# Decoder layer in fp32: cross-attention probabilities and values exchanged between partitions through DRAM instead of inside SBUF, with the division moved

## What is computed

```python
        sim = jnp.einsum('bhid,bjd->bhij', q, k) + mask[:, None, :, :]
        attn = jax.nn.softmax(sim, axis=-1)
        out = jnp.einsum('bhij,bjd->bhid', attn, v)
        out = out.transpose(0, 2, 1, 3).reshape(b, n, INNER) @ Wout
        h = xn @ W1
        val, gate = jnp.split(h, 2, axis=-1)
        out = out + jax.nn.silu(gate) * val @ W2
```

## Time and profile before

| | |
|---|---|
| median of 3 runs | 2093.75 us (2090.76 to 2095.71) |
| profiled execution | 2093.83 us |
| its span, first to last instruction | 2092.0 us |
| TensorE busy | 1724.8 us (82%) |
| VectorE busy | 1346.2 us (64%) |
| ScalarE busy | 974.7 us (47%) |
| DMA engines, mean busy share | 37.1% |

### The profile page before, as it was taken

How to read it: one execution, slowest core, us unless ns; L and a number is a source line. 1 busy time by engine, 2 the same in 40 slices (tenths; PEclk the granted TensorE clock), 3 DMA queues, 4 the chain that set the end, 5 groups by cost and what they waited for, 6 DMA issues and landing times. The chain is left out here.

```text
span 2092.0 us, 25897 instructions
## 1 busy us (share of the span) xinstructions
PE 1724.8 (82%) x7880; PEld 908.4 (43%) x7880; DVE 1346.2 (64%) x3972; ACT 974.7 (47%) x2262; POOL 419.4 (20%) x569
## 2 busy tenths in 40 slices
PE   5579999999996668878878877887888787888786
PEld 2447676676663223333333333333433333333355
DVE  6888999899656555655466465556646656564643
ACT  3355445544335455445455544545544554453541
POOL 4867686768500100000000000000000000000000
PEclk8789999999997879989899989999999999899998
DMA  3000000000144654545454554544554455454531
GB/s 126 1 18 10 27 10 27 19 28 2 35 147 117 185 125 118 130 103 127 121 130 108 142 117 116 133 118 120 124 127 112 117 125 128 107 124 116 118 82 37
DMA packets 153005, 197.33 MB, mean 94 GB/s; under 512 B 56513, under 2 KB 113793, under 8 KB 151969
## 3 DMA queue, kind: packets, MB, share of 16 engines
q1 hardware_dynamic: 152400, 195.21, 37.1%
q10 hardware_dynamic: 464, 0.46, 0.1%
HBM read 96.92 MB, written 7.42 MB: 50 GB/s over the span
## 5 line engine op out<-in xcount | busy, mean ns | idle before, releaser
L1749 ACT ACTIVATE x_pr<-x_pr,x_mx 128x375 f32<-128x375 f32 x448 | 268.3, 599 | 493.4 <-DVE x_mx L1875 493.4
L1875 DVE CUSTOM_DVE_ANT_0 x_pr<-ps,x_mk 128x375 f32<-128x375 f32 x448 | 227.4, 545 | 266.0 <-issue 141.8
L1554 PE MATMUL ps<-x_xn,x_w 128*128 128x448 f32 x512 | 255.1, 634 | 89.8 <-DVE x_so L1962 37.6
L1755 ACT ACTIVATE x_pr<-x_pr,x_rc 128x375 f32<-128x375 f32 x448 | 244.2, 592 | 4.1 <-DVE x_rc L1881 4.1
L1530 PE MATMUL ps<-x_pT,x_va 128*64 128x512 f32 (+1 forms) x768 | 176.6, 600 | 65.5 <-DMA x_pT<-x_blk 65.5
L1892 DVE STREAM_TRANSPOSE x_blk<-x_pr 128x384 f32<-128x384 f32 x448 | 227.8, 547 | 0.0
L1513 PE MATMUL ps<-x_kT,x_qT 64*128 64x375 f32 x896 | 208.7, 545 | 2.6 <-issue 2.4
L1554 PEld LDWEIGHTS ps<-x_xn,x_w 128*128 128x128 f32 x512 | 103.4, 216 | 211.3 <-issue 99.9
L314 PE MATMUL ps<-m_xa,w_in 128*128 128x448 f32 x352 | 146.5, 564 | 6.2 <-ACT m_xa L532 6.2
L1905 DVE TENSOR_TENSOR x_cT<-x_cT,x_rb 128x375 f32<-128x375 f32 x64 | 32.0, 541 | 163.9 <-DMA x_rb<-context_roots 163.9
L1554 PE MATMUL ps<-f_xn,f_w 128*128 128x448 f32 x224 | 100.4, 577 | 39.3 <-DVE x_ff L1947 21.0
(11 more groups left out here) (194 smaller groups left out, 2817.3 us busy)
## 6 DMA issues: line engine op xcount, KB each, us to landing
x_pT<-x_blk SPq DMA_DIRECT2D x512, 96.0 KB, 2.1
x_mk<-in_mask SPq DMA_DIRECT2D x224, 187.5 KB, 4.5
x_pT<-x_blk SPq DMA_DIRECT2D x512, 72.0 KB, 2.1
x_cx<-in_context SPq DMA_DIRECT2D x32, 375.0 KB
x_cT<-in_context_turned SPq DMA_DIRECT2D x32, 375.0 KB, 5.1
x_rb<-context_roots SPq DMA_DIRECT2D x32, 187.5 KB, 5.3
x_va<-x_vT SPq DMA_DIRECT2D x256, 12.0 KB, 1.8
m_Rd<-bc_roots SPq DMA_DIRECT2D x8, 448.0 KB, 3.5
```

The source lines that it names most:

```text
L1554: last = pe.matmul(to[:, 0:T], weights[:, k, at:at + 128], moving[:, k, :], start=(k == 0), stop=(k == KD - 1))
L1749: act.activation(pr[:, k, 0:J], pr[:, k, 0:J], ACT.Exp, scale=-1.0, bias=mx[:, k:k + 1], accum_out=sums[:, k:k + 1]).then_inc(h_e.sem, 1)
L1755: act.activation(pr[:, k + e, 0:J], pr[:, k + e, 0:J], ACT.Copy, scale=rc[:, k + e:k + e + 1]).then_inc(h_n.sem, 1)
L1875: dve.tensor_tensor_reduce(pr[:, k + e, 0:J], bank(2 * (p % 2) + e)[:, 0:J], mk[:, p % SLOT, :], -1.0, 3.0e38, ALU.add, ALU.min, mx[:, k + ...
```

## The change

- The blocks that VectorE turned no longer go from SBUF to SBUF. `blocks_out(p - 2)` stores each step's blocks to a DRAM buffer with one DMA (128 partitions x 4 runs of 768 bytes), and `blocks_in(p - 3)` loads a batch back with four DMAs (32 partitions x 4 runs of 3072 or 2304 bytes each). `blocks` becomes a ring of 3 steps, and `pT` and the DRAM buffer have two copies, so that a load waits for the V product before the last one only.
- The values take the same way: 2 stores (`values_out`, at r = 6) and 2 loads (`values_in`, at r = 0 of the next context) in place of 8 DMAs.
- VectorE's order in a step becomes `highest(p)`, `turn(p - 1)`, the pieces, `divide(p)`; ScalarE's `scaled(p - 1)`, `exps(p)`, the pieces. So the turn comes one step earlier.

```diff
-        def turned_across(i, p):
+        def blocks_out(i, p):
+
+            m = i * STEPS + p
+            sp.wait_ge(h_t.sem, h_t.value(i, 2 * p + 2))
+            if p % NP in (0, NV):
+                hold(sp, h_o, i, batch(p) - 1)
+            sp.dma_start(turned_dram[batch(p) % NB][:, :, p % NP % NV, :].rearrange("q p x -> p q x"),
+                         blocks[:, m % STAGES, :].rearrange("p (q x) -> p q x", q=RB)).then_inc(l_ps[m % STAGES].sem, 16)
+
+        def blocks_in(i, p):
             if p % NP not in (NV - 1, NP - 1):
                 return
...
+            for k in range(p - STAGES + 1, p + 1):
+                told(sp, l_ps, i, k)
+            hold(sp, h_o, i, n - 1)
+            for q in range(RB):
+                sp.dma_start(pT[n % NB][BLK * q:BLK * q + BLK].rearrange("p r s t w b -> p r (s t w b)"),
+                             turned_dram[n % NB][q].rearrange("(r a) s x -> a r (s x)", a=BLK)).then_inc(l_pt.sem, 16)
...
+                if p >= 2 or not first:
+                    blocks_out(*back(it, p, 2))
                 if p >= 3 or not first:
-                    turned_across(*back(it, p, 3))
+                    blocks_in(*back(it, p, 3))
...
         def group(it, first=False, last=False):
             for p in range(STEPS):
-                exps(it, p)
                 if p >= 1 or not first:
                     scaled(*back(it, p, 1))
+                exps(it, p)
...
         def turn(i, p):
...
+            m = i * STEPS + p
+            told(dve, l_ps, 0, m - STAGES)
+            to = blocks[:, m % STAGES, :].rearrange("p (c w b) -> p c w b", w=2, b=BLK)
...
                 highest(it, p)
                 if p >= 1 or not first:
-                    divide(*back(it, p, 1))
-                if p >= 2 or not first:
-                    turn(*back(it, p, 2))
+                    turn(*back(it, p, 1))
...
+                divide(it, p)
```

More of the change, by code:

```diff
@@ L1060 @@
 LAG = 5
-PARTS = RB * RB
+SW = 2 * JW
 CONTEXT = (0, 1, 4)
-VPARTS = DH // BLK * RB
+VPARTS = DH // BLK
+STAGES = 3
 CROOT = 2 * JT + 1 + RSQRT
@@ L1187, in norm_apply, with attention @@
         dve.tensor_scalar(dst(b), src(b), mv[:, b, 0:1], y[:, b:b + 1], ALU.subtract, ALU.mult).then_inc(done.sem, 1)
-def attention(nc, ctx0, PS, apart, ident, xm_dram, ctx_dram, ctx_turned, roots_dram, mask_dram, out_dram, w):
+def attention(nc, ctx0, PS, apart, ident, xm_dram, ctx_dram, ctx_turned, roots_dram, turned_dram, values_dram, mask_dram, out_dram, w):
     sb = Arena(nc, ARENA_AT)
@@ L1220, in attention @@
     rc = sb("x_rc", [ROWS, 2 * SLOT])
-    blocks = [sb(f"x_blk{n}", [ROWS, JW * 2 * width]) for n, width in enumerate((NV, NP - NV))]
-    pT = sb("x_pT", [128, JW * 2 * NV])
+    blocks = sb("x_blk", [ROWS, STAGES, SW])
+    pT = [sb(f"x_pT{n}", [128, RB, width, JC, 2, BLK]) for n, width in enumerate((NV, NP - NV))]
     OT = [sb("x_OT0", [128, GB, KA * S])]
@@ L1255, in attention @@
     c_t = count("c_t", GB)
-    l_pt = count("x_lpt", 16 * PARTS * NB * GB)
+    l_ps = [count(f"x_lps{n}", 0) for n in range(STAGES)]
+    l_pt = count("x_lpt", 16 * RB * NB * GB)
+    l_vs = count("x_lvs", 16 * VPARTS * GB)
     l_rs = count("x_lrs", 16 * GB)
@@ L1328, in batch, with told @@
         return p // NP * NB + p % NP // NV
-    def width_of(n):
-        return 2 * (NV if n % 2 == 0 else NP - NV)
+    def told(eng, sems, i, p):
+        m = i * STEPS + p
+        if m >= 0:
+            eng.wait_ge(sems[m % STAGES].sem, 16 * (m // STAGES + 1))
     def half(ap, h):
@@ L1389, in turned_in, with values_out @@
             sp.dma_start(cT[:, :, :], ctx_turned[i * GB + b, :, :].rearrange("(k p) j -> p k j", p=128)).then_inc(l_ct.sem, 16)
+        def values_out(i, b):
+            sp.wait_ge(c_t.sem, c_t.value(i, b + 1))
+            for k in range(DH // BLK):
+                sp.dma_start(values_dram[:, :, k, :].rearrange("q y x -> y q x"),
+                             vT[BLK * k:BLK * k + BLK, :].rearrange("p (q x) -> p q x", q=RB)).then_inc(l_vs.sem, 16)
         def values_in(i, b):
-            sp.wait_ge(c_t.sem, c_t.value(i, b + 1))
+            sp.wait_ge(l_vs.sem, l_vs.value(i, 16 * VPARTS * (b + 1)))
             hold(sp, h_o, i, NB * (b - 1))
             for k in range(DH // BLK):
-                for q in range(RB):
-                    sp.dma_start(va[BLK * q:BLK * q + BLK, b % 2, :, BLK * k:BLK * k + BLK],
-                                 vT[BLK * k:BLK * k + BLK, q * JC * BLK:(q + 1) * JC * BLK].rearrange("p (t d) -> p t d", d=BLK)).then_inc(l_va[b % 2].sem, 16)
-        def turned_across(i, p):
+                sp.dma_start(va[:, b % 2, :, BLK * k:BLK * k + BLK],
+                             values_dram[:, :, k, :].rearrange("q y (t x) -> (q y) t x", x=BLK)).then_inc(l_va[b % 2].sem, 16)
+        def blocks_out(i, p):
[6 more added lines that the diff above has]
+        def blocks_in(i, p):
             if p % NP not in (NV - 1, NP - 1):
@@ L1445, in group @@
                 b, r = divmod(p, NP)
+                if r == 0 and not (first and b == 0):
+                    values_in(it, b)
                 if last and b == GB - 1:
@@ L1485, in sync @@
         tokens_out(LAST - 2)
+        values_out(0, 0)
         values_in(0, 0)
@@ L1490, in sync @@
         group(NG - 1, last=True)
-        turned_across(NG - 1, STEPS - 1)
+        for p in (STEPS - 2, STEPS - 1):
+            blocks_out(NG - 1, p)
+            blocks_in(NG - 1, p - 1)
+        blocks_in(NG - 1, STEPS - 1)
         for h in range(2):
@@ L1883, in turn @@
         def turn(i, p):
[L1885 to L1889, removed]
+            m = i * STEPS + p
+            told(dve, l_ps, 0, m - STAGES)
+            to = blocks[:, m % STAGES, :].rearrange("p (c w b) -> p c w b", w=2, b=BLK)
             for e in range(2):
                 dve.wait_ge(h_n.sem, h_n.value(i, 2 * p + e + 1))
-                dve.transpose(to[:, :, 2 * (r % NV) + e, :], pr[:, 2 * (p % SLOT) + e, :].rearrange("p (c b) -> p c b", b=BLK)).then_inc(h_t.sem, 1)
+                dve.transpose(to[:, :, e, :], pr[:, 2 * (p % SLOT) + e, :].rearrange("p (c b) -> p c b", b=BLK)).then_inc(h_t.sem, 1)
         def context_norm(it, b, stage):
@@ L2057, in vector @@
         group(NG - 1, last=True)
-        turn(NG - 1, STEPS - 2)
+        turn(NG - 1, STEPS - 1)
         end_back(0)
-        divide(NG - 1, STEPS - 1)
         end_norm(0, 0)
-        turn(NG - 1, STEPS - 1)
         end_norm(0, 1)
@@ L2078, in program @@
     roots = nc.dram_tensor("context_roots", (JP, JT), FP32, kind="Internal").ap()
+    turned_blocks = [nc.dram_tensor(f"turned_blocks{n}", (RB, ROWS, width, JC * 2 * BLK), FP32, kind="Internal").ap() for n, width in enumerate((NV, NP - NV))]
+    turned_values = nc.dram_tensor("turned_values", (RB, BLK, DH // BLK, JC * BLK), FP32, kind="Internal").ap()
     with ExitStack() as ctx:
@@ L2085, in program @@
         mix = mixer(nc, ctx, PS, ident, i_in, x, xm, bc_roots, w)
-        att = attention(nc, ctx, PS, apart, ident, xm, ctx_dram, ctx_turned, roots, mask_dram, out, w)
+        att = attention(nc, ctx, PS, apart, ident, xm, ctx_dram, ctx_turned, roots, turned_blocks, turned_values, mask_dram, out, w)
         block = ctx.enter_context(nc.Block())
```

7 lines of the change are left out of this document (3 added, 4 removed).

## The result

The change makes the kernel faster: 1956.97 us median of 4 runs (1951.0 to 1963.72) against 2093.28 us, ratio 0.935 (95% interval 0.9308 to 0.9392), 136 us. The forecast was 1927 us, with 1860 to 2015 as its range: right in sign and 30 us too low, and the mechanism that it put first, SyncE's issue time, turned out to be about half of the gain.

What follows compares the result with a forecast made beforehand. The prediction took SyncE's issue time to close the loop that holds most contexts, with TensorE busy 80% in the steady part. Its terms summed as 2093.8 - 82 - 50 - 15 - 20 = 1927 us, range 1860 to 2015.

Steps and rivals of the forecast that it cites:

- SyncE's issue time closes the loop: In SyncE's queue, issuing 16 exchange DMAs takes 10.08 us; the loop of 41.7 us holds most contexts of 44.7 us.
- Term 1: The context's roots through DRAM: they leave earlier, saving 82 of TensorE's 100.5 us of waits, bounds 25 to 110.
- lands at about 1293: In one context, `roots_out` could go at 1287.1, queues behind the second batch's four loads, and lands at about 1293 us.
- the round trip stays: Rival: bursts of loads and stores ahead of the roots keep three quarters of the roots' saving away; 2009 us, chance 0.12.
- Term 2: TensorE's wait for exchanged probabilities (`x_pT`) before the products: loads land 2 to 4 us earlier, saving 50 of 65.5 us.
- products wait for their DRAM pair: Rival: store and load through DRAM take 1.9 us more on 64 products, 122 us; 2049 us, chance 0.06.
- Term 3: New order on VectorE and ScalarE: scaling fills ScalarE's idle time, tanh comes up to 1.1 us earlier, saving 15 us.
- a store is a step old by then: In SyncE's queue, the new wait ahead of the loads holds back `roots_out`, but stores land in 3.7 us, steps average 6.4.
- Term 4: TensorE's clock after stalls, 0.63, taken as halfway between two levels: 24 stalls with about 1 us slower matmuls, 20 us saved.
- The DMA engines: DMA busy time per context rises from 22.3 to 32.4 us, a share of 0.82 in 39.5 us, called high, yet hidden.
- the DMA rival: Rival: stores at 110 ns per 768-byte packet make the DMA engines the bound and the kernel slower; 2167 us, chance 0.08.
- Lockstep: Rival: VectorE's `turn` waits for `scaled` wherever ScalarE is behind, 0.3 us x 224 = 67 us; 1994 us, chance 0.05.

Runs made afterwards that it cites:

- the order alone: The kernel before with only the new order on VectorE and ScalarE, the exchange untouched: 2071.88 us, ratio 0.9917.
- Exchange alone: The changed kernel with the old order on VectorE and ScalarE put back, exchange and values still through DRAM: 2168.6 us, ratio 1.0395.
- small masks: The changed kernel with mask loads cut to 8 of 375 columns after the first four: 1921.78 us, ratio 0.9199.

## Why the prediction was right, and where it was off

- *SyncE's issue time closes the loop.* Right as a bound that the change removed: putting twelve issues a batch back costs 74 us. The estimate of 9.5 us of issue per context holds: 7 stores at 0.39, 8 loads in two runs of 2.1, four DMAs of about 0.5 make 8.9. Not right as the only thing: with 16 issues a batch the new route and order still gained 66 us.
- *Term 1, 82 us; measured 49.6.* This is the term that was too large. The step at fault is "lands at about 1293": 6 us for `roots_out` behind the loads. It took 8.5 in the rows above, and in total SyncE waits 182.2 us for it. (The step's own sum also gives 1298.3 and 0.6 us, not 1299 and 1.6, which changes little.) That the loads ahead are what holds up the small store is shown twice. With `roots_out` ahead of them SyncE's wait falls to 23.7 us, and the values' stores of 48 KB land in 8.2 us behind four loads and in 1.9 us behind sixteen. The context issued behind it is not the cause: with that moved away SyncE still waits 189.5 us. What in the four loads takes the 2.5 us more stays open. The forecast of the wait itself, under 50, was missed: 70.0. The rival "the round trip stays" holds in part, with 0.4 of term 1 lost, not three quarters.
- *Term 2, 50 us; measured 39.1.* Wait for `x_pT` 26.4, forecast under 25. The time was sized well: 7.2 us for a load to land, and 2.05 us for the four issues, make at most 9.3 from the first issue on, inside the 8.5 to 10.5. But the four issues are not what gave it. With sixteen the wait is 31.6 us already, and with the order alone 64.4, so most of this term belongs to the route and not to the number of DMAs. The rival "products wait for their DRAM pair" did not come in the changed kernel. A wait of that size came with the old order (189.1 us), and there the late turn is the nearer reading, since the changed kernel has the same pair and waits 26.4. The section that the rival names (the Trainium skill, DMA: Bandwidth & Descriptors, Anatomy of one DMA) describes DMAs issued by gpsimd, and all of these are SyncE's. No run here took a receipt apart.
- *Term 3, 15 us.* 18 us alone. But I called the order a small term of its own, and in the arrangements tried it is a condition of the exchange: without it the route costs 79 us. The sentence "a store is a step old by then" rested on the early turn, and I never priced the exchange without it.
- *Term 4, 20 us; measured 44.2.* The sign was right and the size half. The granted clock of 0.63 is not halfway between the two levels (0.5 and 1) but the mean of a stretch: 0.50 from 1214 to 1216 us and 0.76 from 1216 to 1219. The same four matmuls before and after that stall:

```profile
1202.99 1.67 PE L1554 MATMUL ps<-x_xn,x_w 128*128 128x448 f32 x4
1213.85 3.35 PE L1554 MATMUL ps<-x_xn,x_w 128*128 128x448 f32 x4 [5.69 <-DVE x_so L1962]
```

  They lost 1.7 us, not "about 1", and TensorE's 27 waits for products were left out of the count. See also the last section.
- *The DMA engines.* 32.4 us a context forecast; (1777.8 - 810.4) / 24 = 40.3 us a context, from the first and last `roots_out` of 25 between 800 and 1800 us, x 0.79 = 31.8. The price of 45 ns a packet fits: 31.8 - 22.3 = 9.5 us for 224 packets, 42 ns, if the loads cost what the exchange inside SBUF did, which no row tells by itself. The rule of the Trainium skill, Perfetto Trace Analysis, DMA Optimizations, on DMAs under 2 KB did not decide here. It speaks of the size of a DMA; these stores have 384 KB each, in runs of 768 bytes, and the engines did not become the bound that the DMA rival named. "High, yet hidden" was the wrong word all the same, as the smaller masks show.
- *Lockstep* did not show: VectorE waits 1.7 us in all ahead of the transposes for ScalarE.

Against the span, 49.6 + 39.1 + 44.2 = 132.9 of 142.8 us. Term 3 has no share of its own in that, since what the order gave lies in these waits. Of the rest, 4.1 is TensorE's wait behind the gate piece (47.6 before, 43.5 after).

## What to carry to other kernels

Where one queue issues every transfer, add its issue durations around a loop before looking at bytes: 16 small DMAs of 0.63 us were dearer here than a detour through DRAM with twice the bytes, and half of the gain came only when four DMAs did the loading. Then ask what leaves the queue's wait: the queue that was no longer busy issued in bursts, and a short round trip behind a burst took the burst's time. Five reorderings of the transfers were tried, one in the kernel before and four in the changed one. Each lengthened one wait at least, and all four in the changed kernel lost. And undo each part of a combined change by itself, since a part that seems free may be what makes the other one pay.

## What the runs showed that I had not expected

Granted clock and busy time move together in most runs with the same 7880 TensorE instructions. Exchange alone, the kernel before, the changed kernel, small masks: clock 0.899, 0.925, 0.945, 0.952; busy 1756.3, 1724.8, 1680.6, 1669.9 us; spans 2190.5, 2092.0, 1949.2, 1915.3 (2190.5 is the slowest of that kernel's four executions; the others took 2161 to 2167). Busy time times clock is 1579 to 1595 us in all four, so the clock accounts for nearly all of the difference. From the first to the last, 86 of 275 us, 31%, are the same matmuls taking longer; from before to after, 44.2 of 142.8. A wait taken off TensorE went along with half as much again as its own length. Whether idle time is what lowers the clock these runs don't prove, and the order alone departs from the row: a shorter span than before (2078.4), yet a lower clock (0.917) and more busy time (1733.2).

A transfer's landing may depend on what is issued behind it as well as ahead: `x_rb` landed in 4.8 us with masks and stores right behind it, in 5.5 with the context there too, in 4.0 with the masks cut down, and in 10.9 where it was itself behind loads, context, mask and store. Only the last is a large difference, and none of these kernels changed what stands behind alone.
